# First layer's feed-forward block: inner width padded from 32 to 128 with zero weights in both products

## What is computed

```python
D = 128
HID = D // 4                       # 32
def _forward(x, ..., ff_down_w, ff_down_b, ff_up_w, ff_up_b):
    ...                            # causal depthwise convolution, router, 8 experts
    h = _rmsnorm(x1 + moe_out, norm_w)
    ff = jax.nn.gelu(jnp.einsum('bsd,hd->bsh', h, ff_down_w) + ff_down_b, approximate=False)
    ff = jnp.einsum('bsh,dh->bsd', ff, ff_up_w) + ff_up_b
    return h + ff

x = x + _L0_ffn_ref(_layernorm(x, axis=-1), ...)
```

## Time and profile before

| | |
|---|---|
| median of 3 runs | 6852.19 us (6822.35 to 6868.85) |
| the profiled execution, its own time | 6882.46 us |
| its span in the trace | 6880.6 us |
| TensorE busy (MATMUL records) | 5494.3 us, 80% |
| VectorE busy | 4304.2 us, 63% |
| GpSimd busy | 3251.0 us, 47% |
| ScalarE busy | 2877.9 us, 42% |
| mean granted TensorE clock | 0.852 of 2.4 GHz |

### The profile page before, as it was taken

One profiled execution on the slowest core, in us unless ns is written; L12 is line 12 of the kernel. 1 busy time (PEld: TensorE's weight loads), 2 busy tenths in 40 slices (PEclk: granted clock), 3 DMA queues, 4 the chain that ended last, 5 costly groups with the idle time before them and its releaser, 6 DMA issues. The chain is left out here.

```text
span 6880.6 us, 81795 instructions
## 1 busy us (share of the span) xinstructions
PE 5494.3 (80%) x22762; PEld 2782.0 (40%) x22762; DVE 4304.2 (63%) x6292; ACT 2877.9 (42%) x4905; POOL 3251.0 (47%) x2381
## 2 busy tenths in 40 slices
PE   5888888888868887788896888965797688885797
PEld 1333333333324435342584444423564234433465
DVE  5999999999984730565323666753575455553575
ACT  4656666566644532344321444431232244441232
POOL 2888888788863510243211333325433344434433
PEclk8999999999998955887656998986898799995898
DMA  1133111111110000000002232311454333311355
GB/s 66 74 136 135 74 74 68 74 57 73 74 55 0 0 0 0 0 0 0 4 0 52 64 77 65 76 76 60 137 189 133 70 75 73 80 30 56 126 186 176
DMA packets 174785, 476.04 MB, mean 69 GB/s; under 512 B 29648, under 2 KB 54992, under 8 KB 146640
## 3 DMA queue, kind: packets, MB, share of 16 engines
q1 hardware_dynamic: 156272, 434.21, 19.9%
q0 software_dynamic: 18176, 37.79, 1.6%
HBM read 364.81 MB, written 107.07 MB: 69 GB/s over the span
## 5 line engine op out<-in xcount | busy, mean ns | idle before, releaser
L337 POOL TENSOR_TENSOR mamba_bu<-mamba_du,mamba_b_all 128x1024 f32<-128x1024 f32 x512 | 1200.9, 2356 | 280.9 <-DVE mamba_hc L599 269.3
L592 DVE TENSOR_TENSOR_SCAN mamba_bu<-psum,mamba_bu 128x512 f32<-128x512 f32 x1024 | 1192.6, 1205 | 157.2 <-ACT psum L529 124.2
L428 PE MATMUL psum<-mamba_hc,consts 128*128 128x512 f32 x2048 | 1014.7, 620 | 20.5 <-DVE mamba_du L604 20.5
L529 ACT ACTIVATE psum<-mamba_delta,A 128x510 f32<-128x510 f32 x1024 | 684.6, 685 | 572.8 <-DVE mamba_bu L592 558.6
L599 DVE TENSOR_TENSOR mamba_hc<-mamba_bu,psum 128x1024 f32<-128x1024 f32 x512 | 611.2, 1194 | 6.0 <-PE psum L419 6.0
L428 PEld LDWEIGHTS psum<-mamba_hc,consts 128*128 128x128 f32 x2048 | 402.9, 198 | 368.9 <-issue 349.6
L1598 POOL DMA_INDIRECT results<-ffn_moe_y_rows,ffn_moe_row_of x312 | 302.0, 968 | 508.8 <-DVE ffn_moe_y_rows L1788 433.2
L2363 POOL TENSOR_TENSOR loc_q_bd<-loc_q_max,weights_l1a 128x512 fp32r<-128x512 f32 x256 | 274.9, 1102 | 543.6 <-DVE loc_q_max L2597 526.1
L1713 ACT ACTIVATE ffn_moe_act<-ffn_moe_act 128x512 f32<-128x512 f32 x344 | 216.9, 631 | 722.8 <-DVE ffn_moe_act L1757 722.7
L2427 PE MATMUL psum<-consts 128*128 128x256 bf16 (+1 forms) x1024 | 284.9, 320 | 235.6 <-issue 175.5
L419 PE MATMUL psum<-mamba_parts,consts 128*128 128x512 bf16 x512 | 201.7, 394 | 334.4 <-DVE mamba_hc L599 332.4
(11 more groups left out here) (395 smaller groups left out, 11779.8 us busy)
## 6 DMA issues: line engine op xcount, KB each, us to landing
mamba_b_all<-b_rows SPq DMA_DIRECT2D x128, 1024.0 KB, 6.3
ffn_moe_w_gu<-gate_up_parts SPq DMA_DIRECT2D x78, 1024.0 KB, 4.8
pairs<-empty_rows SPq DMA_DIRECT2D x6, 3432.0 KB, 15.3
ffn_moe_got<-pairs SPq DMA_DIRECT2D x78, 264.0 KB, 3.2
ffn_moe_w_down<-in_l_moe SPq DMA_DIRECT2D x78, 256.0 KB, 2.9
qk_rows<-loc_qk SPq DMA_DIRECT2D x16, 1024.0 KB, 13.5
ffn_moe_back<-results SPq DMA_DIRECT2D x32, 512.0 KB, 4.6
qk_rows<-cau_qk SPq DMA_DIRECT2D x16, 1024.0 KB, 6.1
```

The lines of the kernel that those rows point to most:

```text
L337: nc.gpsimd.tensor_tensor(bu[:, J % BU, :, :], du[:, q % 2, :, :], b, ALU.mult).then_inc(bu_ready, 1)
L428: nc.tensor.matmul(ysum[h], mem.ident, hc[:, J % HC, h, :], start=(n == 0), stop=(n == NST - 1), skip_group_check=True).then_inc(summed, 1)
L529: nc.scalar.activation(by_seq(dA[i % DECAYS])[:, :, 1:S], by_seq(delta[:, q % 2, h, :])[:, :, 1:S], ACT.Exp, scale=mem.A[:, q % 2, h * NST ...
L592: nc.vector.tensor_tensor_scan(bu[:, J % BU, h, :], dA[i % DECAYS], bu[:, J % BU, h, :], 0.0, ALU.mult, ALU.add).then_inc(scanned, 1)
```

## The change

In both products the inner width is filled up from 32 to 128. The down weight gets 96 zero columns, its bias 96 zeros, the up weight 96 zero rows; `g` and the written part of the PSUM bank grow from 32 to 128 partitions. A padded inner value is gelu(0 + 0) = 0 and meets a zero weight, so the result is the same sum. `weights_l` grows from 1859 to 1955 float32 columns. The number of instructions, their order on every engine and all waits stay as they are.

```diff
@@ l0_feed_forward
-        g = ctx.enter_context(nc.sbuf_tensor(stage + "_g", [HID, 2, T], F32))
+        g = ctx.enter_context(nc.sbuf_tensor(stage + "_g", [D, 2, T], F32))
...
-                nc.tensor.matmul(mem.bank[s][0:HID, :], w["down"], U[:, cols(t)], start=True, stop=True,
-                                 ).then_inc(down_ready, 1)
+                nc.tensor.matmul(mem.bank[s], w["down"], U[:, cols(t)], start=True, stop=True).then_inc(down_ready, 1)
...
-                nc.scalar.activation(g[:, s, :], mem.bank[s][0:HID, :], ACT.Gelu, bias=w["down_b"]).then_inc(g_ready, 1)
+                nc.scalar.activation(g[:, s, :], mem.bank[s], ACT.Gelu, bias=w["down_b"]).then_inc(g_ready, 1)
@@ pack_l0
-        "down": f("ff_down_w").T, "down_b": col(f("ff_down_b")), "up": f("ff_up_w").T, "up_b": col(f("ff_up_b")),
+        "down": np.pad(f("ff_down_w").T, ((0, 0), (0, D - HID))), "down_b": col(np.pad(f("ff_down_b"), (0, D - HID))),
+        "up": np.pad(f("ff_up_w").T, ((0, D - HID), (0, 0))), "up_b": col(f("ff_up_b")),
```

## The result

| | before | changed |
|---|---|---|
| median of 20 runs each | 6854.98 us (6819.45 to 6893.37) | 6816.28 us (6763.57 to 6832.4) |
| ratio, 95% interval | | 0.994 (0.9922 to 0.9958) |
| span of the profiled execution | 6880.6 us | 6815.2 us |
| mean granted clock | 0.852 | 0.858 |
| first feed-forward, first product to last sum | 63.53 us | 37.68 us |

The changed kernel is 38.7 us faster in the timed runs, 0.6%. The prediction was 6801 us. Its saving of 50.8 us was 12 us too large against the timed runs. The two profiled executions are 65.4 us apart, more than the forecast and more than the stages account for (49.7 us), so one pair of executions doesn't settle the size.

The account below looks back on a forecast made before the run. The prediction took TensorE at 1.2 GHz to bound the feed-forward stages. Savings of 25.6 us twice, 51.2, less 0.2 and 0.2 of costs gave -50.8 us: 6852.2 to 6801 us, range 6775 to 6838.

Parts of the forecast that it names:

- TensorE at 1.2 GHz bounds the stage: Feed-forward before the change: TensorE at half clock sets the pace, 7.69 us a pair of tiles, 63.5 us a stage.
- The clock rises: Both feed-forward stages: padding raises TensorE's clock to near 1.00, giving 6801 us; chance 0.80.
- what differs is the part of the array that the products fill: 128*32 and 32*128: Feed-forward against neighbouring stages: narrow products go with clock 0.50, the neighbours' 128*128 products with a higher clock.
- The third stage that was called as a witness: Another stage with 32-row products, busy 20.00 of 20 us, cited as also having clock 0.50.
- 4.15 us a pair: Two feed-forward tiles after the change: 3.16 us even-tile chain through the table load plus 0.99 us for up.
- Covered weight loads: Feed-forward products: with both at 128*128, weights load under the preceding product, so 0.43 us a tile of exposed loads goes.
- The start of a stage: First feed-forward tiles run cold, the clock rising after about 5.1 us; the stage ends at 37.9 us.
- The stage behind stays cold: Layer norm after the feed-forward: no inherited high clock counted; inheriting it would save 2.6 us twice.
- From the stages to the whole: Whole program: 51.2 us stage saving less small costs gives 50.8 us off the timed median, everything outside unchanged.

Follow-up runs that it names:

- before_preload: The kernel before with the gelu table loaded once ahead of the tile loop, nothing padded: 6884.94 us beside 6902.93, ratio 0.9965.
- padded_preload: The changed kernel with the gelu table loaded once ahead of the tile loop: 6848.58 us, ratio 0.9912 to the kernel before.
- down_only: The kernel before with only the down product's output widened to 128 columns, gelu and up left at 32: 6878.91 us beside 6863.15, ratio 1.001.
- width64: The kernel before with both products padded to an inner width of 64 (128*64 and 64*128): 6885.4 us beside 6863.15, ratio 1.0016.
- up_only: The kernel before with only the up product padded to 128 rows, g cleared once, down left at 128*32: 6854.13 us, one run.
- filler: The kernel before, 32 wide, with one more 128*128 product a tile that nobody reads: 6895.59 us, ratio 0.9991.
- filler_rows: The kernel before with one more 128*32 product a tile that nobody reads: 6841.75 us, one run, beside a median of 6847.42.
- the two repetitions: The changed kernel with only blank lines added, timed twice more beside the kernel before: 6868.4 and 6801.37 us, ratio 0.9948 each.

## Why the prediction was right, point by point

**TensorE at 1.2 GHz bounds the stage.** Right. `before_preload` takes 9 us a stage of ScalarE's work away (seven of eight table loads), and the pair stays at 7.69 us.

**The clock rises.** Right, in both stages of every trace of the changed kernel. That most of the weights were zeros didn't hinder it. The reason given for it was only half right. The step "what differs is the part of the array that the products fill: 128*32 and 32*128" treats rows and columns alike. The runs show that the 32 columns of `down` never held the clock down, and that widening it alone costs 4.8 us. With one of two products reading 32 rows (or 64) the clock stayed at 0.50, and more rows for `up`, or one more product of 128 rows a tile, raised it. The forecast came out because the change pads both; that it pads the right one too is luck. The third stage that was called as a witness, 3340 to 3360 us, isn't made of 32-row products alone: by the trace 64*128 and 128*64 products take turns with them.

**4.15 us a pair.** 4.19 measured. ScalarE starts 1.12 us after `down` (2410.34 to 2411.46), where the layer norm gave 1.06; `up` behind a wait takes 0.96 instead of 0.99. `padded_preload` confirms that the table load was what ended last.

**Covered weight loads.** Right for every product that doesn't wait. The first load is in the open wherever two neighbours differ in shape and one of them has 32 or 64 rows or columns (before, `down_only`, `width64`, `up_only`, `filler`), and covered with equal shapes and between 128*96 and 96*128. The extra product of `filler_rows`, 128*32 like the `down` before it, starts 0.88 us behind it, with its load (2416.16) under it; the `up` of this kernel, 32*128, starts 0.95 us behind the extra product, with its first load in the open (2414.66):

```profile
2413.71 1.02 PE L1067 MATMUL psum<-U,consts 128*32 x2
...
2414.66 0.29 PEld L1072 LDWEIGHTS psum<-ffn_ff_g,weights_l 32*128 32x128 f32 x2 [0.84 <-issue]
...
2415.71 1.04 PE L1065 MATMUL psum<-U,weights_l 128*32 x2
...
2416.16 0.11 PEld L1067 LDWEIGHTS psum<-U,consts 128*32 128x32 f32 x1 [0.32 <-issue]
2416.59 1.02 PE L1067 MATMUL psum<-U,consts 128*32 x2
```

By the Trainium skill ("TensorEngine Tiling (Array Packing)", Key Properties) a change of tiling mode drains the engine. These loads agree with that; a drain by itself stands in no row.

**The start of a stage.** 37.9 us predicted, 37.7 and 39.7 found. I let the clock rise about 5 us behind the first product. In the first stage it rose earlier, 3.7 us behind it (0.50 to 2404.7, 1.00 from 2404.9), and `up(0)` runs at full speed. In the second it rose later, about 9 us behind it (0.50 to 3176, 1.00 from 3176.5), and `up(0)` and `down(2)` still take 1.86 and 1.70 us to the next product.

```profile
3171.68 2.07 PE L1070 MATMUL psum<-ffn_ff_g,weights_l 128*128 128x512 f32 x2 [0.50 <-ACT ffn_ff_g L1086]
3173.54 1.91 PE L1065 MATMUL psum<-U,weights_l 128*128 x2
3175.24 1.06 PE L1070 MATMUL psum<-ffn_ff_g,weights_l 128*128 128x512 f32 x1
```

The saving was to be 51.2 us and is 25.85 + 23.81 = 49.7. It came this close because one rise was early and the other late; what makes a stage fall on one side or the other, the traces don't show.

**The stage behind stays cold.** Right. Its first six records take 5.46 us behind the first feed-forward, against 5.42 in the earlier trace rows, and 5.20 behind the second, against 5.39 before.

**From the stages to the whole.** Here the forecast is too large. The sum was 50.8 us off the median and 38.7 were measured, 35 and 46 in the two repetitions. The stage terms are within 2 us in every trace, so 11 of the 12 us lie outside the stages. The prediction put everything outside at no change; whether that term is wrong or the medians strayed stays open, since the part of the program behind varies by more than this from trace to trace.

## What to carry to other kernels

Read a stage's granted clock beside its busy share before counting its instructions: a stage that is 94% busy can run at half speed, and products with few contraction rows (partitions read) in the mix may be the reason. Padding the contraction side with zeros cost nothing in streaming here: from `up` to the next `down` it is 2.00 us with 32 rows and with 64 (`width64`), both at 1.2 GHz. Padding the output side alone only lengthened the weight load, by 0.15 us a tile (`down_only`). And when an engine is made twice as fast, look up at once who stands next; here it was a table load that one line removes.

## What the hardware showed beyond expectation

An extra 128*32 product a tile, work for nothing, made a stage 12.6 us shorter (50.96 against 63.53 us), with the granted clock at 0.99 from 2410 to 2450 us; a 32*128 product of the same area left the clock at 1.2 GHz and made the stage 27 us longer. Worth knowing too: the built program had a table load inside the loop, 1283 ns eight times a stage, with no other table in use there, and it cost only about 0.55 us a stage until TensorE became faster.
